# The last group of a fused decoder layer turned by TensorE, and another written order of its period

## The reference, cut to what matters

```python
# x: 4 x 1024 x 256 float32, 16 heads of 16 channels, state of 64, context of 77 rows, hidden width 1024
x = layernorm(x + mamba(x))        # per head: XBC = silu(W x + b), A = exp(cum_i - cum_j) below the diagonal,
                                   # Y = (A * (C B^T)) X;  out = (gate * Y) @ W_out.T + b_out
x = layernorm(x + xattn(x, ctx))   # softmax(q k^T / 4, masked) v, 16 heads, 77 keys, then a projection
x = layernorm(x + ffn(x))          # relu(x W1 + b1) W2 + b2
```

## Time and profile before

| | us |
|---|---|
| median of 3 runs | 686.73 |
| lowest and highest | 681.88, 687.03 |
| the profiled execution | 682.82 |
| its span, first to last instruction | 681.1 |
| TensorE busy | 635.5 (93%), 8314 matmuls |
| VectorE busy | 545.9 (80%) |
| GpSimd busy | 482.1 (71%) |
| ScalarE busy | 450.6 (66%) |
| mean granted clock of TensorE | 0.974 of full speed |

### The profile page before, as it was taken

The page is one execution under the profiler, slowest core; times in us unless marked ns, Lnnn a source line. Parts: engine busy times, 40 slices in busy tenths (PEclk is TensorE's granted clock), DMA queues, the critical chain, the costliest instruction groups (busy, mean ns, idle before and its releaser), DMA issues.

```text
span 681.1 us, 22040 instructions
## 1 busy us (share of the span) xinstructions
PE 635.5 (93%) x8314; PEld 542.2 (80%) x8314; DVE 545.9 (80%) x1325; ACT 450.6 (66%) x1105; POOL 482.1 (71%) x774
## 2 busy tenths in 40 slices
PE   6989988889999999999999999999999999998786
PEld 4667766678888888888888888888888888977675
DVE  2377778988888898989898888988888989989422
ACT  4967747778677686868686786868686765233221
POOL 1343656677869686877878696868778786968765
PEclk7799978989999999999999999999999999999989
DMA  3421454444344444444443454445344535455410
GB/s 110 175 72 27 130 136 109 121 130 123 103 123 129 119 127 124 131 99 117 134 127 107 121 138 114 129 125 136 81 127 133 129 86 129 123 144 142 142 47 33
DMA packets 91271, 79.22 MB, mean 116 GB/s; under 512 B 47517, under 2 KB 85789, under 8 KB 91165
## 3 DMA queue, kind: packets, MB, share of 16 engines
q1 hardware_dynamic: 90749, 77.52, 42.6%
q10 hardware_dynamic: 416, 0.28, 0.1%
HBM read 43.37 MB, written 33.55 MB: 113 GB/s over the span
## 4 chain that ended last, share of the span: by engine, by line
PE 73%; DVE 11%; ACT 6%; POOL 5%; issue 3%; DMA 1%; ACTq 0%; POOLq 0%; DVEq 0%
PE bank L492 12%; PE bank L480 11%; PE bank L356 9%; PE bank L300 4%; PE bank L459 4%; PE bank L417 4%; PE bank L428 4%; PE bank L370 3%; PE bank L469 2%; PE bank L446 2%; POOL hl L1348 2%; PE bank L284 2%; PE bank L343 2%; PE bank L312 2%; PE bank L397 2%
## 5 line engine op out<-in xcount | busy, mean ns | idle before, releaser
L1324 POOL TENSOR_TENSOR P<-P,rc 128x308 f32<-128x308 f32 x128 | 86.0, 699 | 25.9 <-DVE rc L1127 25.9
L993 DVE TENSOR_TENSOR E<-bank,E 128x512 f32<-128x512 f32 x128 | 81.8, 680 | 21.7 <-PE bank L356 21.1
L492 PE MATMUL bank<-w2h,hh 128*128 128x256 f32 x256 | 75.7, 296 | 9.0 <-POOL hl L1348 8.9
L1348 POOL TENSOR_TENSOR hl<-hr,hh 128x512 fp32r<-128x512 f32 x64 | 81.9, 1289 | 0.3
L1284 POOL TENSOR_SCALAR_AFFINE_SELECT E<-E 128x508 f32<-128x508 f32 x128 | 80.1, 650 | 0.0
L356 PE MATMUL bank<-Cc,Bc 64*128 64x128 f32 x1024 | 73.7, 290 | 4.6 <-DVE cmat L976 3.6
L356 PEld LDWEIGHTS bank<-Cc,Bc 64*128 64x128 f32 x1024 | 64.4, 195 | 15.0 <-issue 5.8
L745 ACT ACTIVATE E<-bank 128x512 f32<-128x512 f32 x128 | 68.1, 599 | 11.0 <-PE bank L343 10.6
L492 PE MATMUL bank<-w2h,hl 128*128 128x256 f32 x256 | 72.3, 283 | 0.0
L492 PE MATMUL bank<-w2l,hh 128*128 128x256 f32 x256 | 72.3, 282 | 0.0
L797 ACT ACTIVATE hr<-bank,cst 128x256 f32<-128x256 f32 x128 | 54.4, 495 | 26.8 <-PE bank L480 14.3
(11 more groups left out here) (114 smaller groups left out, 1781.0 us busy)
## 6 DMA issues: line engine op xcount, KB each, us to landing
turn_p<-TP SPq DMA_DIRECT2D x128, 160.0 KB, 2.8
PT<-turn_p SPq DMA_DIRECT2D x32, 640.0 KB, 4.3
xr<-in_x SPq DMA_DIRECT2D x32, 128.0 KB, 2.6
turn_x<-xr SPq DMA_DIRECT2D x128, 32.0 KB, 1.8
tT<-turn_x SPq DMA_DIRECT2D x32, 128.0 KB, 2.7
turn_x<-x SPq DMA_DIRECT2D x128, 32.0 KB, 2.0
xu<-turn_x SPq DMA_DIRECT2D x32, 128.0 KB, 3.1
out<-res SPq DMA_DIRECT2D x32, 128.0 KB, 2.7
```

The lines of the kernel that those rows point to most:

```text
L492: i = eng.matmul(bk[:, 0:256], hm[:, m, cols(n)], wm[:, m, :], start=m == 0 and k == 0, stop=m == 7 and k == 2)
L993: eng.tensor_tensor(E[:, h % 4, r, :, :], b_g[n, u, r][:, :].rearrange("p (h t) -> p h t", h=4), E[:, h % 4, r, :, :], ALU.mult).then_inc( ...
L1324: eng.tensor_tensor(v, v, rc[:, n % 2, 4 * j:4 * j + 4].unsqueeze(2).to_broadcast([128, 4, S]), ALU.mult).then_inc(p_norm, 1)
L1348: eng.tensor_tensor(hl[:, 2 * j:2 * j + 2, :], hr[:, j % 2, :, :], hh[:, 2 * j:2 * j + 2, :].bitcast(F), ALU.subtract).then_inc(h_rest, 1)
```

## The change

For the last group, tiles 30 and 31 (`is_last`), the block transposes and the DMAs through DRAM go; TensorE transposes x1, P and x2 against the identity into PSUM (2, 10 and 2 transposes for each tile), and ScalarE copies the result to tT, PT and xu (1, 3 and 1 copies). For this group VectorE also makes the division of the softmax (`n_last`) and the low part of x2 (`u_last`), and for the groups 14 and 15 the low part of the hidden values (`h_last`); GpSimd made these before. Waits of `soft_sub` are fitted to it.

Besides, the lists of all five engines are replaced, prologue, period and tail. The period keeps its functions and the tiles of each stage, in another order: `pv` and `attn_proj` of tile 2s-6, `score(2s-4)`, both `diff` of tile 2s-1 and `y(2s-2)` now stand in the second half of round s (they opened the next). In the prologue `warm(0)` stands behind `bc(0, 1)` where it was first, and `pv(0)`, `score(2)` and `y(4)` precede the loop. SyncE's loop has one round more (s = 18) and its puts and gets another order: `put_x2(2s-6)` is last in a round, `get_x2(2s-9)` comes behind it in the next.

The diff, cut to the new functions and, of the lists, to the new side of the period and of the tail (TensorE, ScalarE, VectorE, GpSimd, SyncE, in this order; lines that were there before in the same sequence have no sign):

```diff
+def is_turned(n):
+
+    return 0 <= n < NT - GT
+
+
+def is_last(n):
+    return NT - GT <= n < NT
 
...
+    def x1_turn(n):
+        if not is_last(n):
+            return
+        bk = b_turn["x1", n] = banks.take(pe, x1T, DMA * (n + 1))
+        pe.wait_ge(ld_cmat, DMA)
+        pe.wait_ge(ln_out[0], n + 1)
+        for h in range(2):
+            i = eng.transpose(bk[:, 128 * h:128 * h + 128], x1[:, n % 4, 128 * h:128 * h + 128], ident)
+        i.then_inc(x1_flip, 1)
+
+    def p_turn(n):
+        if not is_last(n):
+            return
+        for c in range(3):
+            b_turn["p", n, c] = banks.take(pe, pT, DMA * (n + 1))
+        for m in range(NBLK):
+            pe.wait_ge(p_norm, 4 * n + 2 * (m // 5) + 2)
+            i = eng.transpose(b_turn["p", n, m // 4][:, 128 * (m % 4):128 * (m % 4) + 128],
+                              P[:, m // 5, 128 * (m % 5):128 * (m % 5) + 128], ident)
+            if m % 4 == 3 or m == NBLK - 1:
+                i.then_inc(p_turned, 1)
+
+    def x2_turn(n):
+        if not is_last(n):
+            return
+        bk = b_turn["x2", n] = banks.take(pe, x2T, DMA * (n + 1))
+        pe.wait_ge(ln_out[1], n + 1)
+        for h in range(2):
+            i = eng.transpose(bk[:, 128 * h:128 * h + 128], x2[:, n % 5, 128 * h:128 * h + 128], ident)
+        i.then_inc(x2_flip, 1)
...
     for s in range(4, 18):
         ffn1(s - 6, range(6, 8))
         gate(2 * s - 4)
         bc(s - 1, 1)
         gmat(2 * s - 3, 0)
         gmat(2 * s - 3, 1)
+        state_turn(2 * s - 4)
+        cum(2 * s - 1)
+        query(2 * s - 5)
         out_proj(2 * s - 4)
+        score(2 * s - 5)
+        diff(2 * s - 2, 0)
+        ffn2(2 * s - 12)
         pv(2 * s - 7)
         state_in(2 * s - 3)
+        inter(2 * s - 3)
+        diff(2 * s - 2, 1)
+        tok(2 * s)
         attn_proj(2 * s - 7)
+        state_turn(2 * s - 3)
+        gate(2 * s - 3)
+        ffn2(2 * s - 11)
+        if s == 17:
+            x1_turn(30)
+        y(2 * s - 3)
+        bc(s, 0)
+        pv(2 * s - 6)
+        gmat(2 * s - 2, 0)
+        out_proj(2 * s - 3)
         ecum(2 * s - 2)
+        ecum(2 * s - 1)
+        cum(2 * s)
         ffn1(s - 5, range(0, 3))
+        query(2 * s - 4)
+        attn_proj(2 * s - 6)
+        diff(2 * s - 1, 0)
+        diff(2 * s - 1, 1)
+        score(2 * s - 4)
+        ffn1(s - 5, range(3, 6))
+        gmat(2 * s - 2, 1)
+        state_in(2 * s - 2)
+        tok(2 * s + 1)
         inter(2 * s - 2)
+        y(2 * s - 2)
+    x1_turn(31)
+    query(31)
     ffn1(12, range(6, 8))
+    pv(29)
+    p_turn(30)
+    attn_proj(29)
     ffn2(24)
+    score(31)
+    pv(30)
+    ffn1(13, range(0, 3))
     ffn2(25)
     ffn1(13, range(3, 6))
+    attn_proj(30)
+    p_turn(31)
     ffn1(13, range(6, 8))
+    pv(31)
     ffn2(26)
     ffn2(27)
+    attn_proj(31)
+    x2_turn(30)
     ffn1(14, range(0, 3))
     ffn1(14, range(3, 6))
     ffn1(14, range(6, 8))
+    x2_turn(31)
     ffn2(28)
     ffn2(29)
...
+    def x1_turn(n):
+        if not is_last(n):
+            return
+        act.wait_ge(q_mm, n)
+        act.wait_ge(x1_flip, n + 1)
+        eng.copy(tT[:, :, :, :].rearrange("p i h b -> p h i b"),
+                 b_turn["x1", n][:, 0:256].rearrange("p (h i b) -> p h i b", h=2, i=4)).then_inc(x1T, DMA)
+
+    def p_turn(n):
+        if not is_last(n):
+            return
+        act.wait_ge(pv_mm, n)
+        for c in range(3):
+            k = 4 if c < 2 else 2
+            act.wait_ge(p_turned, 3 * (n - NT + GT) + c + 1)
+            i = eng.copy(PT[:, :, 4 * c:4 * c + k, :].rearrange("p i m b -> p m i b"),
+                         b_turn["p", n, c][:, 0:128 * k].rearrange("p (m i b) -> p m i b", m=k, i=4))
+        i.then_inc(pT, DMA)
+
+    def x2_turn(n):
+        if not is_last(n):
+            return
+        act.wait_ge(u_lo, n)
+        act.wait_ge(x2_flip, n + 1)
+        eng.copy(xu[:, :, :, :].rearrange("p i h b -> p h i b"),
+                 b_turn["x2", n][:, 0:256].rearrange("p (h i b) -> p h i b", h=2, i=4)).then_inc(x2T, DMA)
...
+    for s in range(4, 18):
+        tok(2 * s - 1)
+        hidden(s - 6, range(6, 8))
+        bc(s - 1, 1)
+        state_turn(2 * s - 4)
+        cum_top(2 * s - 1)
+        query(2 * s - 5)
+        u_top(2 * s - 10)
+        exp_diff(2 * s - 2, 0)
+        o_turn(2 * s - 7)
+        exp_diff(2 * s - 2, 1)
+        p_soft(2 * s - 5)
+        u_top(2 * s - 9)
+        if s == 17:
+            x1_turn(30)
+        tok(2 * s)
         state_turn(2 * s - 3)
+        bc(s, 0)
+        cum_top(2 * s)
+        o_turn(2 * s - 6)
+        ecum(2 * s - 2)
+        ecum(2 * s - 1)
         hidden(s - 5, range(0, 3))
+        query(2 * s - 4)
+        exp_diff(2 * s - 1, 0)
+        exp_diff(2 * s - 1, 1)
         hidden(s - 5, range(3, 6))
         p_soft(2 * s - 4)
+    x1_turn(31)
+    hidden(12, range(6, 8))
+    o_turn(29)
     u_top(26)
+    query(31)
+    p_turn(30)
     u_top(27)
+    o_turn(30)
+    p_soft(31)
     hidden(13, range(0, 3))
     hidden(13, range(3, 6))
+    p_turn(31)
     hidden(13, range(6, 8))
     u_top(28)
+    o_turn(31)
     u_top(29)
     hidden(14, range(0, 3))
+    x2_turn(30)
     hidden(14, range(3, 6))
     hidden(14, range(6, 8))
     u_top(30)
+    x2_turn(31)
     u_top(31)
...
+    def h_last(g, j):
+        if not NG - 2 <= g < NG:
+            return
+        dve.wait_ge(ffn2_mm, GT * g)
+        dve.wait_ge(h_top, 4 * g + j + 1)
+        eng.tensor_tensor(hl[:, 2 * j:2 * j + 2, :], hr[:, j % 2, :, :], hh[:, 2 * j:2 * j + 2, :].bitcast(F),
+                          ALU.subtract).then_inc(h_rest, 1)
+
+    def n_last(n, js):
+        if not is_last(n):
+            return
+        dve.wait_ge(p_rcp, n + 1)
+        for j in js:
+            v = P[:, j // 2, 4 * S * (j % 2):4 * S * (j % 2) + 4 * S].rearrange("p (h s) -> p h s", s=S)
+            eng.tensor_tensor(v, v, rc[:, n % 2, 4 * j:4 * j + 4].unsqueeze(2).to_broadcast([128, 4, S]),
+                              ALU.mult).then_inc(p_norm, 1)
+
+    def u_last(n):
+        if not is_last(n):
+            return
+        k = slice(4 * (n % GT), 4 * (n % GT) + 4)
+        dve.wait_ge(ffn1_mm, 8 * (n // GT))
+        dve.wait_ge(u_hi, n + 1)
+        eng.tensor_tensor(ul[:, k, :, :], xu[:, :, :, :], uh[:, k, :, :].bitcast(F),
+                          ALU.subtract).then_inc(u_lo, 1)
...
     for s in range(4, 19):
         ln3_out(2 * s - 13)
+        x1_blocks(2 * s - 5)
         cum_rest(2 * s - 2)
+        ln2_stats(2 * s - 8)
         soft_sub(2 * s - 6, range(0, 2))
         soft_sub(2 * s - 6, range(2, 4))
+        a_times_g(2 * s - 4, 1)
         state_add(2 * s - 4)
         soft_sum(2 * s - 6)
+        if s == 18:
+            n_last(30, range(0, 2))
+            n_last(30, range(2, 4))
+        y_decay(2 * s - 4)
         ln2_out(2 * s - 8)
         log_a(2 * s - 1)
         x2_blocks(2 * s - 8)
+        y_out(2 * s - 4)
+        p_blocks(2 * s - 6, 0)
+        p_blocks(2 * s - 6, 1)
         a_times_g(2 * s - 3, 0)
         a_times_g(2 * s - 3, 1)
+        cum_rest(2 * s - 1)
         ln1_stats(2 * s - 4)
         soft_sub(2 * s - 5, range(0, 2))
         soft_sub(2 * s - 5, range(2, 4))
+        ln3_stats(2 * s - 12)
+        state_add(2 * s - 3)
+        ln1_out(2 * s - 4)
+        y_decay(2 * s - 3)
+        x1_blocks(2 * s - 4)
+        ln2_stats(2 * s - 7)
+        soft_sum(2 * s - 5)
+        if s == 18:
+            n_last(31, range(0, 2))
+            n_last(31, range(2, 4))
+        log_a(2 * s)
         ln2_out(2 * s - 7)
         x2_blocks(2 * s - 7)
         y_out(2 * s - 3)
+        ln3_stats(2 * s - 11)
+        p_blocks(2 * s - 5, 0)
+        ln3_out(2 * s - 12)
+        p_blocks(2 * s - 5, 1)
+        ln1_stats(2 * s - 3)
         a_times_g(2 * s - 2, 0)
+        ln1_out(2 * s - 3)
+    ln2_stats(30)
+    ln3_stats(26)
     ln3_out(25)
+    ln2_out(30)
     ln3_stats(27)
     ln3_out(26)
     ln2_stats(31)
+    h_last(14, 0)
+    h_last(14, 1)
+    ln2_out(31)
+    h_last(14, 2)
+    h_last(14, 3)
+    u_last(30)
     ln3_out(27)
+    u_last(31)
     ln3_stats(28)
     ln3_stats(29)
+    h_last(15, 0)
     ln3_out(28)
+    h_last(15, 1)
+    h_last(15, 2)
     ln3_out(29)
+    h_last(15, 3)
...
     for s in range(4, 17):
+        x_resid(2 * s - 2)
+        h_hi(s - 5, 1)
+        h_hi(s - 5, 2)
+        h_low(s - 5, 1)
         decay(2 * s - 1, 0)
         soft_norm(2 * s - 4, range(0, 2))
+        soft_norm(2 * s - 4, range(2, 4))
         decay(2 * s - 1, 1)
+        h_low(s - 5, 2)
+        h_hi(s - 5, 3)
+        h_low(s - 5, 3)
+        u_rest(2 * s - 8)
         x2_bias(2 * s - 7)
+        x2_bias(2 * s - 6)
+        ln1_rstd(2 * s - 2)
         ln3_rstd(2 * s - 10)
         x_resid(2 * s - 1)
         decay(2 * s, 0)
+        u_rest(2 * s - 7)
         ln2_rstd(2 * s - 5)
         soft_norm(2 * s - 3, range(0, 2))
         soft_norm(2 * s - 3, range(2, 4))
+        ln3_rstd(2 * s - 9)
         decay(2 * s, 1)
```

(39 more changed lines are left out.)

523 lines of the change are left out of this document (175 added, 348 removed).

## The result

The changed kernel takes 688.02 us (median of 20 runs, 684.03 to 695.7), the former one 683.43 us beside it (20 runs): ratio 1.0067, 95% interval [1.0039, 1.0095]. It is slower by 0.7%, within 1%, where 3.6 us less were forecast.

What follows compares the result with a forecast made beforehand. TensorE's own work was taken to bind the steady rounds, with idle time in prologue and tail. Profiled 682.8 - 2.1 (tail) + 0 (period) - 1.5 (prologue) = 679.2 us, or 683.1 on the median's scale; range 672 to 693.

Steps and rivals of the forecast that it cites:

- The prologue, -1.5 us: Prologue, 0 to 160 us: the new order was to win 1.5 us, from -8 to +5.
- pv(0): Prologue: pv(0) stands later by several groups and was to lose its idle time of 2.5 us.
- warm(0): Prologue: its eight matmuls, now after bc(0, 1) in a half-clock stretch, were to cost 1 us, up to 3.4.
- The period, 0: Steady rounds: one 0.3 us gap replaces another of that size, so 0 us, from -3.6 to +11.
- The tail, -2.1 us: Tail: gaps -6.7, transposes +4.3, waits for GpSimd +0.3, together -2.1 us, from -9 to +8.
- The 28 transposes: Tail, TensorE: the new transposes of tiles 30 and 31 were to add 4.3 us, between 3.1 and 7.
- query(31): Tail, TensorE: a 4.4 us idle wait for the copy x1_turn(31) behind the softmax, 2.9 to 6.
- out_proj(31): Tail, TensorE: a wait of 1.7 us for y_out(31) on VectorE, 0 to 3.
- ffn1(13): Tail: a 0.6 us wait, 0 to 2, as get_x2(27) stands behind put_x2(28) in SyncE's list.
- The shared port: Rival, tail: VectorE's 18 new instructions sit out GpSimd's, +4 us, 687 us; chance 0.12.
- VectorE sets the period: Rival, steady rounds: VectorE's chain to gmat(2s-3, 1) exceeds TensorE's, slower, 695 us; chance 0.14.
- tail and prologue close: Rival: gaps in tail and prologue shrink and the period's gap goes, -13.9 us, 673 us; chance 0.29.

Runs made afterwards that it cites:

- e1: The changed kernel with warm(0) moved back in front of tok(0) on TensorE: ratio 1.0079 to the former kernel.
- e2: The former kernel with warm(0) moved behind bc(0, 1) on TensorE: ratio 0.9995 to the former kernel.
- e14: The changed kernel with GpSimd's split_w(0) behind decay(2, 0) instead of ahead of it: ratio 0.9994 to the former kernel.
- e17: The former kernel with GpSimd's split_w(0) behind decay(2, 0) instead of ahead of x_resid(1): ratio 1.0045 to the former kernel.
- e13: The changed kernel with TensorE's warm(1) ahead of ecum(2) instead of behind score(0): ratio 1.0090 to the former kernel.
- e5: The changed kernel with its prologue calls in the former kernel's order on all five engines, period and tail kept: ratio 1.0193 to the former kernel.
- e3: The changed kernel with x1_turn(31) on ScalarE ahead of p_soft(30), and ln3_stats(24) and ln2_stats(29) on VectorE ahead of soft_sub(31): ratio 1.0071 to the former kernel.
- e6: The changed kernel with the low part of the hidden values of groups 14 and 15 on GpSimd again: ratio 1.0184 to the former kernel.
- e15: The kernel of e8 with GpSimd's split_w(0) behind decay(2,1) instead of ahead of x_resid(1): ratio 0.9973 to the former kernel.
- e8: The former kernel's prologue and period with the new path of tiles 30 and 31 and a tail rewritten for it: ratio 0.9926 to the former kernel.
- e16: The kernel of e8 run once more, unchanged, beside e15: ratio 0.9962 to the former kernel.

## Why the prediction was wrong, and where it was right

**The prologue, -1.5 us: the step that failed.** It was forecast to win 1.5 us and lost some 4 by the medians (4.6, with nothing from the period and 0.2 from the tail) and 10.7 by the profiles. Of what was named, pv(0) did lose its wait of 2.5 us, and warm(0) was worth nothing (e1, e2). What decided was not looked for: which instructions of VectorE and GpSimd the new order brings side by side. The prediction had the rule and its row and applied them only to the 18 new instructions in the tail; besides, it told the rule for two SBUF inputs alone, which the products do not have. VectorE's products became 3.0 us longer, TensorE waited 2.3 us, and its clock fell for the 17 us behind that, worth 8 us in this profile. In other profiles of the same prologue the stretch is shorter, which goes with medians that differ by less than the two profiles. e14 and e17 show from both sides that the meeting of split_w(0) and the products costs the time. That TensorE's wait brings the low clock is likely, since it came behind the wait in all eight profiles that have it and not in e14, but no run separated the two, since e13 failed; and the clock also falls without such a wait (e5, half clock from 57.8 to 61.2 us, with no wait over 0.5 us in the 15 us ahead of it). Nor is it shown that the collision is the whole of the loss: the interval of e14 reaches from 0.4% under the former kernel to 0.2% over it. The range of the step, -8 to +5, held the medians' result but not the profiles'.

**The period, 0: right.** 150.5 us from y(20) to y(28) in both, 37.6 a round. VectorE does not set it.

**The tail, -2.1 us: its size was wrong, near 0 in fact.** The 28 transposes hold TensorE for 3.1 us from their starts to what follows (4.3 expected, 3.1 was the lower end). query(31) waits 4.51 us (4.4 expected), and e3 shows that the softmax on VectorE stands behind it, as the count had it. n_last takes 0.47 us (0.48 expected), h_last 0.69 (0.65 expected) but for two, and GpSimd's gaps went; e6 prices them at 6 us or more (four gaps of 6.1 us together). From y(28) on the gaps come to 11.6 us, before to 13.9: 2.3 us less, where 6.7 less were counted. out_proj(31) waits 0.38 instead of 1.7, but before ffn1(13) there is a wait of 3.23 us in place of 0.6: its bank is the one that attn_proj(29) took eight places earlier, which ln2_stats(29) frees, and this stands behind soft_sub(31) and ln3_stats(24) on VectorE. The prediction followed operands there and forgot the bank. The rest of the account from y(28) on: 2.3 us less of gaps, 3.1 more of transposes, 1.8 more of half clock (6.8 us of it in place of 3.3). Measured is 0.2 more, so 2.4 us went elsewhere; most of it is in ffn2, where before each wait for hl a matmul stands in the trace with its full 0.28 us, while otherwise the next starts 0.12 us after it.

**The rivals.** The shared port was a rival with its place wrong: in the tail two of the 18 instructions sat out GpSimd's, the last two h_last, 1.22 us each in place of 0.69, which cost no more than the 0.77 us before the last block of ffn2 (0.3 expected); the great part came in the prologue. The upper end of the tail's range, +8, leaves this port's 4 us out, which changes nothing here. That VectorE sets the period, and that tail and prologue close, did not come.

## What to carry to other kernels

A new order of the lists makes instructions neighbours that never met: for every GpSimd instruction of a microsecond or more that reads SBUF, a copy as well as a difference, look up what VectorE does from SBUF to SBUF at that moment, old code included. And a call moved on one list may hold up another: in e15 the load behind split_w(0) kept SyncE's queue. A stretch at half clock is to be read from its beginning: what matters is the wait ahead of it. And a wait on TensorE is followed through the bank ring as well as through the operands; a filler that takes a bank waits too.

## What had not been expected of the hardware

The same kernel, profiled twice (e8, then e16), had its half-speed stretches at different places. Busy time and clock of the first 30 us, e8:

```profile
0.00:30.00 30.00, 23.15 (x192) 16.34 (x192) 9.50 (x34) 19.59 (x56) 7.45 (x16) 0.72 0.47 159
```

and e16:

```profile
0.00:30.00 30.00, 23.91 (x154) 17.28 (x154) 7.64 (x30) 17.89 (x54) 6.77 (x15) 1.00 0.46 159
```

The one with the whole clock had made less by then (y(0) at 33.6 us against 30.0), and their spans are 679.6 and 673.5 us. So a few microseconds between two single profiles say little about an edit, in this kernel above all in its first 160 us; the timed rounds decide, and a profile is for finding the instruction.
